# A tuned adaLN block: a third buffer for queries, keys, values and gates, the first projections ahead of the late modulation columns, and new orders on every engine

## The reference

```python
mod = (silu(c) @ wmod).reshape(4, 6, 1, 256)        # shift, scale, gate, twice
sa, ca, ga, sb, cb, gb = mod[:, 0], ..., mod[:, 5]  # ga and gb kept away from 0
h = layernorm(x) * (1 + ca) + sa
q, k = rope(h @ Wq.T), rope(h @ Wk.T)               # 4 heads of 32
v, g = h @ Wv.T, silu(h @ Wg.T)                     # 4 heads of 64
# retention: causal, with decay gamma per head, state S (32 x 64) per head
o = rms_norm_per_head(retention(q, k, v)) * gnorm_w
x = x + ga * ((o * g) @ Wo.T)
h = layernorm(x) * (1 + cb) + sb
x = x + gb * (fwht(silu(h @ W1.T) * (h @ W3.T)) @ W2.T)   # hidden width 1024
```

## Time and profile before

| | us |
|---|---|
| median of 3 runs | 286.54 |
| lowest and highest | 286.5, 286.86 |
| the profiled execution, its own time | 287.58 |
| its span, first to last instruction | 285.4 |
| TensorE busy in the span | 258.5 (91%) |
| VectorE, GpSimd, ScalarE busy | 173.6, 138.1, 122.0 |

### The profile page before, as it was taken

How to read it: one execution, slowest core, us unless ns; L and a number is a source line. 1 busy time by engine, 2 the same in 40 slices (tenths; PEclk the granted TensorE clock), 3 DMA queues, 4 the chain that set the end, 5 groups by cost and what they waited for, 6 DMA issues and landing times.

```text
span 285.4 us, 5010 instructions
## 1 busy us (share of the span) xinstructions
PE 258.5 (91%) x1888; PEld 240.7 (84%) x1888; DVE 173.6 (61%) x340; ACT 122.0 (43%) x249; POOL 138.1 (48%) x159
## 2 busy tenths in 40 slices
PE   1696797789999999999999999999998999899992
PEld 1564585679889989999999998999998999799992
DVE  2317777899696675747476786658458555572210
ACT  2414545476247324723473146623454344233320
POOL 2066226415745491474728383755166627542632
PEclk9999689999999999999999999999999999999998
DMA  6997300100010002000200002000100011001011
GB/s 191 383 379 271 147 2 1 37 3 0 2 37 1 2 0 57 20 2 1 75 1 2 0 0 76 0 3 0 40 32 5 2 37 39 0 0 39 5 34 37
DMA packets 11294, 14.02 MB, mean 49 GB/s; under 512 B 1156, under 2 KB 9220, under 8 KB 11016
## 3 DMA queue, kind: packets, MB, share of 16 engines
q1 hardware_dynamic: 11272, 13.71, 14.5%
HBM read 9.77 MB, written 2.11 MB: 42 GB/s over the span
## 4 chain that ended last, share of the span: by engine, by line
PE 68%; DVE 11%; POOL 8%; issue 4%; DMA 4%; ACT 2%; SPq 2%; POOLq 0%; DVEq 0%; ACTq 0%
PE pu L298 25%; PE pacc L298 13%; PE pd L298 5%; PE pa L298 4%; PE pb L298 4%; DMA wmod_sb<-wmod 3%; PE pc L305 3%; DVE xn L622 2%; PE pc L298 2%; POOL rso L784 2%; PE pacc L348 2%; POOL qk L809 1%; POOL hid_lo L830 1%; PE pstate L298 1%; PE pstate L323 1%
## 5 line engine op out<-in xcount | busy, mean ns | idle before, releaser
L298 PE MATMUL pu<-h_hi,w_hi 128*128 128x256 f32 x256 | 73.1, 286 | 0.0
L298 PE MATMUL pu<-h_hi,w_lo 128*128 128x256 f32 x256 | 72.4, 283 | 0.0
L298 PE MATMUL pu<-h_lo,w_hi 128*128 128x256 f32 x256 | 72.4, 283 | 0.0
L830 POOL TENSOR_TENSOR hid_lo<-hid,hid_hi 128x512 fp32r<-128x512 f32 x32 | 43.1, 1350 | 34.9 <-ACT hid_hi L772 34.8
L298 PEld LDWEIGHTS pu<-h_hi,w_hi 128*128 128x128 f32 x256 | 49.0, 191 | 0.4
L298 PEld LDWEIGHTS pu<-h_lo,w_hi 128*128 128x128 f32 x256 | 49.0, 191 | 0.3
L298 PEld LDWEIGHTS pu<-h_hi,w_lo 128*128 128x128 f32 x256 | 49.0, 191 | 0.0
L298 PE MATMUL pacc<-w_hi,hid_hi 128*128 128x256 f32 x128 | 37.6, 294 | 0.7 <-POOL hid_lo L830 0.7
L298 PE MATMUL pacc<-w_lo,hid_hi 128*128 128x256 f32 x128 | 36.2, 282 | 0.0
L298 PE MATMUL pacc<-w_hi,hid_lo 128*128 128x256 f32 x128 | 36.1, 282 | 0.0
L767 ACT ACTIVATE silu<-pu 128x512 f32<-128x512 f32 x32 | 19.0, 594 | 31.6 <-PE pu L298 31.2
...
## 6 DMA issues: line engine op xcount, KB each, us to landing
...
```

The costliest lines, as they stand in the source:

```text
L298: mm = pe.matmul(ps, a, c, start=start and n == 0, stop=stop and n == len(ops) - 1, skip_group_check=True)
L830: pool.tensor_tensor(hid_lo[:, k % 2], hid32[:, k % 2], hid_hi[:, k % 2].bitcast(F32), ALU.subtract).then_inc(p_hid.sem, 1)
```

## The change

`E_BUFS = 3` buffers for `k_hi`, `k_lo`, `v2`, `gg` and `qkt`, indexed by `buf = u % E_BUFS`; ScalarE's waits go to readers of unit u-3. Room is made by four edits: `rope_a` is gone (VectorE writes into `qk`, and GpSimd adds `rope_b` in place; the waits for the readers of the unit before go from GpSimd's `rope` to VectorE's), `y0` is gone (`yo` is scaled in place, after the square is taken), `sq` shares memory with `tmp`, and the block mask of the state shrinks from 256 columns to 4, read as a broadcast. Among the loads, the second part of `wmod` goes behind `w2`, the constants and the second rotation table. The orders of all five engines are rewritten.

```diff
+E_BUFS = 3
-C_CAUSAL, C_HADAMARD, C_BLOCKS, C_END = 0, P, 2 * P, 2 * P + HEADS * DV
+C_CAUSAL, C_HADAMARD, C_BLOCKS, C_END = 0, P, 2 * P, 2 * P + HEADS
     "SP": steps(
-        "0:rows 1:qb 2:qb 3:qb 0:out 1:out 4:qb 5:qb 2:out 6:qb 3:out 7:qb 4:out 5:out 6:out 7:out"),
+        "0:rows 1:qb 2:qb 3:qb 4:qb 5:qb 6:qb 0:out 7:qb 1:out 2:out 3:out 4:out 5:out 6:out 7:out"),
     "PE": steps(
-        "0:cols 0:ht 0:cols.1 0:rows 0:qk 0:vg 0:qkt 0:vg.1 0:sc 0:sc.1 1:ht 0:had 0:st 0:had.1 0:o 1:qk 1:vg "
+        "0:cols 0:ht 0:qk 0:vg 0:rows 0:cols.1 0:qkt 0:vg.1 0:sc 0:sc.1 1:ht 0:st 0:had 0:had.1 1:qk 0:o 0:st.1 "
...
-        rope_a, rope_b, qk = (sb(n, [P, 2, QK]) for n in ("rope_a", "rope_b", "qk"))
-        v2 = sb("v2", [P, 2, 2, HEADS, 2, DV], F32R)
+        qk, rope_b = (sb(n, [P, 2, QK]) for n in ("qk", "rope_b"))
+        v2 = sb("v2", [P, E_BUFS, 2, HEADS, 2, DV], F32R)
...
-        yo, y0, sq, tmp, xn2 = (sb(n, [P, 2, D]) for n in ("yo", "y0", "sq", "tmp", "xn2"))
+        yo, tmp, xn2 = (sb(n, [P, 2, D]) for n in ("yo", "tmp", "xn2"))
+        sq = tmp
...
             load_x(1)
+            sp.dma_start(raw_w2[:], w2).then_inc(in_w2.sem, 16)
+            sp.dma_start(cst[:], consts).then_inc(in_cst.sem, 16)
+            sp.dma_start(trig_sb[:, 1], trig[:, 1]).then_inc(in_trig[1].sem, 16)
             sp.dma_start(wmod_sb[:, :, 2 * D:6 * D], wmod[:, :, 2 * D:6 * D]).then_inc(in_mod2.sem, 16)
-            sp.dma_start(cst[:], consts).then_inc(in_cst.sem, 16)
-            sp.dma_start(raw_w2[:], w2).then_inc(in_w2.sem, 16)
...
-                    if u >= 2:
-                        act.wait_ge(t_o.sem, t_o.after(u - 2, 1))
+                    if u >= E_BUFS:
+                        act.wait_ge(t_o.sem, t_o.after(u - E_BUFS, 1))
```

More of the change, by code:

```diff
@@ L276, in step @@
                         sp.dma_start(qb[rows, :, :, h, :].rearrange("p e t i -> p (e t) i").bitcast(F32),
-                                     qkt[rows, par, :, :, 0].rearrange("p e t i -> p (e t) i").bitcast(F32)
+                                     qkt[rows, buf, :, :, 0].rearrange("p e t i -> p (e t) i").bitcast(F32)
                                      ).then_inc(s_qb.sem, 16)
@@ L396, in step @@
                         pe.wait_ge(d_br.sem, d_br.after(u - 1))
-                    three(pz[k][:, :], [((qkt[:, par, 0, k, 1], qkt[:, par, 1, k, 1]),
+                    three(pz[k][:, :], [((qkt[:, buf, 0, k, 1], qkt[:, buf, 1, k, 1]),
                                          (qb[:, 0, k], qb[:, 1, k]))]).then_inc(t_s.sem, 1)
@@ L405, in step @@
                         pe.wait_ge(d_cols.sem, 2)
-                    three(pstate[:, 0:HEADS * DV], [((k_hi[:, par, k], k_lo[:, par, k]),
-                                                     (v2[:, par, k, :, 0], v2[:, par, k, :, 1]))],
+                    three(pstate[:, 0:HEADS * DV], [((k_hi[:, buf, k], k_lo[:, buf, k]),
+                                                     (v2[:, buf, k, :, 0], v2[:, buf, k, :, 1]))],
                           start=(t == 0)).then_inc(t_kv.sem, 1)
@@ L413, in step @@
                         pe.wait_ge(p_s.sem, states(u, k))
-                        three(out_k[:, :, 0], [((qkt[:, par, 0, k, 0], qkt[:, par, 1, k, 0]),
+                        three(out_k[:, :, 0], [((qkt[:, buf, 0, k, 0], qkt[:, buf, 1, k, 0]),
                                                 (s_hi[:, (t - 1) % 2], s_lo[:, (t - 1) % 2]))], stop=False)
@@ L418, in step @@
                     for h in range(HEADS):
-                        pe.matmul(out_k[:, h], p_hi[:, k, h], v2[:, par, k, h], start=(t == 0 and h == 0), stop=False,
+                        pe.matmul(out_k[:, h], p_hi[:, k, h], v2[:, buf, k, h], start=(t == 0 and h == 0), stop=False,
                                   skip_group_check=True)
-                        mm = pe.matmul(out_k[:, h, 0], p_lo[:, k, h], v2[:, par, k, h, 0], start=False,
+                        mm = pe.matmul(out_k[:, h, 0], p_lo[:, k, h], v2[:, buf, k, h, 0], start=False,
                                        stop=(h == HEADS - 1), skip_group_check=True)
@@ L554, in step @@
                     dve.wait_ge(a_vg.sem, a_vg.after(u, k))
-                    split(d_vlo, v2[:, par, k, :, 1], heads(pa[:, 0:D]), v2[:, par, k, :, 0])
+                    split(d_vlo, v2[:, buf, k, :, 1], heads(pa[:, 0:D]), v2[:, buf, k, :, 0])
                 elif kind == "qklo":
                     dve.wait_ge(a_qkt.sem, a_qkt.after(u))
-                    split(d_qklo, qkt[:, par, 1].rearrange("p t q n -> p (t q n)"), pb[:, :],
-                          qkt[:, par, 0].rearrange("p t q n -> p (t q n)"))
+                    split(d_qklo, qkt[:, buf, 1].rearrange("p t q n -> p (t q n)"), pb[:, :],
+                          qkt[:, buf, 0].rearrange("p t q n -> p (t q n)"))
                 elif kind == "qb" and u == 0:
@@ L564, in step @@
                         rows = slice(h * DK, (h + 1) * DK)
-                        ins = dve.tensor_copy(qb[rows, 1, :, h, :], qkt[rows, par, 1, :, 0].bitcast(F32))
+                        ins = dve.tensor_copy(qb[rows, 1, :, h, :], qkt[rows, buf, 1, :, 0].bitcast(F32))
                     ins.then_inc(d_qb0.sem, 1)
@@ L697, in step @@
                     act.wait_ge(t_vg.sem, t_vg.after(u, k))
-                    if u >= 2:
-                        act.wait_ge(t_o.sem, t_o.after(u - 2, 1))
-                        act.wait_ge(p_y0.sem, p_y0.after(u - 2, 1))
-                        act.wait_ge(t_kv.sem, states(u - 2, 0) + 2 - (u - 2) % 2)
-                    act.activation(v2[:, par, k, :, 0], heads(pa[:, 0:D]), ACT.Copy)
-                    act.activation(gg[:, par, k], pa[:, D:2 * D], ACT.Silu).then_inc(a_vg.sem, 1)
+                    if u >= E_BUFS:
+                        act.wait_ge(t_o.sem, t_o.after(u - E_BUFS, 1))
+                        act.wait_ge(p_y0.sem, p_y0.after(u - E_BUFS, 1))
+                        act.wait_ge(t_kv.sem, states_through(u - E_BUFS))
+                    act.activation(v2[:, buf, k, :, 0], heads(pa[:, 0:D]), ACT.Copy)
+                    act.activation(gg[:, buf, k], pa[:, D:2 * D], ACT.Silu).then_inc(a_vg.sem, 1)
                 elif kind == "qkt":
                     act.wait_ge(t_qkt.sem, t_qkt.after(u))
-                    if u >= 2:
-                        act.wait_ge(t_o.sem, t_o.after(u - 2, 1))
-                    act.activation(qkt[:, par, 0].rearrange("p t q n -> p (t q n)"), pb[:, :], ACT.Copy
+                    if u >= E_BUFS:
+                        act.wait_ge(t_o.sem, t_o.after(u - E_BUFS, 1))
+                    act.activation(qkt[:, buf, 0].rearrange("p t q n -> p (t q n)"), pb[:, :], ACT.Copy
                                    ).then_inc(a_qkt.sem, 1)
@@ L714, in step @@
                         rows = slice(h * DK, (h + 1) * DK)
-                        ins = act.activation(qb[rows, 0, :, h, :], qkt[rows, par, 0, :, 0].bitcast(F32),
+                        ins = act.activation(qb[rows, 0, :, h, :], qkt[rows, buf, 0, :, 0].bitcast(F32),
                                              ACT.Copy)
@@ L739, in step @@
                     if u:
-                        act.wait_ge(d_ss.sem, d_ss.after(u - 1, k))
+                        act.wait_ge(d_x1.sem, d_x1.after(u - 1))
                     act.activation(sq[:, k], yo[:, k], ACT.Square).then_inc(a_sq.sem, 1)
@@ L818, in step @@
                 elif kind == "ss":
-                    pool.wait_ge(d_o.sem, d_o.after(u, k))
-                    if u:
-                        pool.wait_ge(t_yt.sem, t_yt.after(u - 1))
-                    pool.tensor_tensor(y0[:, k], yo[:, k], gg[:, par, k], ALU.mult).then_inc(p_y0.sem, 1)
+                    pool.wait_ge(a_sq.sem, a_sq.after(u, k))
+                    pool.tensor_tensor(yo[:, k], yo[:, k], gg[:, buf, k], ALU.mult).then_inc(p_y0.sem, 1)
                     pool.wait_ge(d_ss.sem, d_ss.after(u, k))
```

50 lines of the change are left out of this document (25 added, 25 removed), and 90 rows, old and new, of the table ORDERS.

## The result

| | before | changed |
|---|---|---|
| median of 4 runs, us | 286.52 (286.5 to 286.86) | 276.21 (275.44 to 276.75) |
| ratio to before, 95% interval | | 0.963 (0.9609 to 0.9651) |
| profiled execution, its own time | 287.58 | 275.44 |
| its span | 285.4 | 273.5 |

The profiled span is 11.9 shorter.

A forecast was written before the change was run, and what follows sets the result against it. TensorE, busy for 91% of the span, was taken as the bound, with time to win mostly in the first 60 us. The terms -2.2 - 1.5 - 1.0 = -4.7 gave 281.8 us, range 278.2 to 285.2.

The forecast's parts named there:

- which stay: From qkt to the first scores: 4.78 us, made of ScalarE's and VectorE's copies, would stay unchanged.
- at the same price: After the first scores: the clock falls again, costing some 3.3 us as before; bounds -3.3 and +3.3.
- 2.95 in all, and no more is to be had: After the first up: TensorE's four remaining waits, 0.59, 0.37, 0.85 and 1.14 us, limit the gain.
- Part 1: Start until the first scores: -2.2 us, scores at 27.9 instead of 30.05.
- near 20.6: At the start: the clock rises there, during rows and cols.1, so qkt begins at 23.1; bounds 22.0 and 25.5.
- Part 2: From the first scores to the first up: -1.5 us, bounds 0 and -2, from fewer waits.
- in one piece, 2.9 us: Ahead of the first scores: TensorE pauses once, from near 25.0 until 27.9, so the clock is expected to fall.
- Rival B: After the first scores: the clock doesn't fall, 278.5 us; chance 20%.
- Part 3: From the first up to the end: -1.0 us, two waits gone for -2.0, against new ones; bounds -2.95 and +2.
- two new waits: Between qkt and sc of unit 5 and between proj and h2t of unit 2: less cover, +0.5 us each.
- rival D: Scores of units 3 to 5: block-query transfers late, three stalls, 288.4 us at 2.2 each; chance 8%.
- The in-place output: Among the memory edits: changes no count or size of a product, its readers are done earlier; 0 us.

The follow-up runs named there:

- e1: The changed kernel with two buffers instead of three, all orders, loads and memory edits kept: 277.18 us, 0.9667 of before.
- e8: The changed kernel with the late modulation columns moved behind unit 0's second vg, VectorE's part behind its copies, GpSimd's butterflies ahead of kspl: 276.19 us, 0.9647 of before.
- e9: The changed kernel run again unchanged: 276.42 us, 0.9657 of before.
- e6: The kernel before, with only GpSimd's second round of w2 butterflies moved ahead of its rotation: 285.43 us, 0.9956 of before.
- e7: The changed kernel, with GpSimd's second round of butterflies held back until VectorE's remainder of unit 0's queries is done: 279.45 us, 0.9746 of before.
- e5: The kernel before, with 14 extra products filling TensorE's three pauses ahead of the first scores: 287.17 us, 1.0022 of before.
- e11: The kernel before with one edit, yo scaled in place, so GpSimd's product waits for ScalarE's square: 288.59 us, 1.0058 of before.
- e12: The kernel before with the new orders from qkt of unit 5 on, on every engine but SyncE: 287.55 us, 1.001 of before.
- e4: The changed kernel with before's orders and loads up to the first up, and the new orders behind it: 283.21 us, 0.9874 of before.
- e2: The changed kernel's three buffers and memory edits with before's orders and order of loads: 287.67 us, 1.0037 of before.
- e13: As e12, with ScalarE's and VectorE's part of unit 5's queries also as far ahead as in the changed kernel: 283.26 us, 0.9853 of before.
- e10: As e8, with VectorE's gates also moved behind the values' remainder: 278.28 us, 0.9703 of before.
- e14: The changed kernel with two buffers and y0 back, so GpSimd's product no longer waits for the square: 276.01 us, 0.9607 of before.

## Where the prediction held, and which of its steps failed

The prediction was wrong in its size. The direction and the mechanism of the three parts held, but 276.21 us lies below the range, and in the profiles the gain is 11.9 us, where the sum has 4.7. Three terms failed: the copies ahead of the first scores, "which stay", shrank by 1.4; the low clock, expected again "at the same price" of 3.3, did not come, and costs 1.6 where it does; and of the waits after the first `up`, "2.95 in all, and no more is to be had", 3.6 was had.

**What held.** `ht` stood at 9.32 (9.7 forecast), `qk` at 13.01 (13.3) with starts 0.21 apart, `vg` ended near 18.4 (18.5) at the low clock, and the late `wmod` was hidden. The third buffer is worth nothing (e1). "qkt, on which the scores hang, still stands behind both groups that were overtaken" was the right brake, and e8 shows the next one behind it, VectorE.

**Part 1: -4.6 instead of -2.2.** Three terms were off. The first, 0.3, is the landing of the first weights (5.92 against 6.19), which differs from run to run by more than that. The second, 0.7, is the rise of the clock. The text took it "near 20.6", as before; it came at 18.5, with the end of `vg`, so both overtaken groups ran at the full clock and `qkt` began at 22.09, at the lower of its two bounds. Even that is no bound: in e9 the products of `vg` start 0.23 apart from 16.18 on, no longer 0.43, and `qkt` is at 21.07. The third, 1.4, failed outright: "made of ScalarE's and VectorE's copies, which stay". They went from 4.78 to 3.37, since GpSimd's last butterfly had ended as the copies began (e6 and e7 show it from both sides). GpSimd's second round stands behind its rotation in both orders. The rotation came 6.0 us earlier (17.96 against 23.96) and the copies only 3.2, so GpSimd was through. What was not asked is which other engine is at work while a timed row runs.

**Part 2: -3.35 instead of -1.5.** The order itself was sized well. Without a low stretch the old orders need 28.5 (e5, e6, e11, e12), the new ones 26.8: -1.75. The rest, 1.6, is the low clock. Two steps of that failed. The pause was to be "in one piece, 2.9 us" and was 1.34, since the copies took 1.4 less; and a long single pause doesn't bring the fall in any case (e7, 3.29 us without one). And the price of 3.3, half of TensorE's busy time at 1.2 GHz, is twice too high: the old orders lose 1.6 in three profiles with the stretch (30.1 to 30.3 against 28.5) and 0.8 in e4, and over 61 executions of before 0.7. Rival B had the event right, and its 278.5 was still too high, because parts 1 and 3 were.

How much of the 1.6 is the change's doing is partly luck. Before's own profile happened to have the stretch, as three other profiles with its start had (e2, e4, e13), but not e6, e11 and e12. Of the eight profiles with the new start only e10 has a fall near the first scores; e7 and e9 have one later, and e9 is the same kernel as the first.

**Part 3: -3.6 instead of -1.0.** "2.95 in all, and no more is to be had" was a wrong bound. It left out a fifth wait, the 0.59 at 257.21 for the norm of unit 7. And the idle column gives less than a stall takes. From the start of the last product ahead to the start of the waiting one, less the usual distance, the five cost 0.76, 0.54, 1.03, 1.31 and 0.75, so 4.4 (an estimate from the trace of before). The forecast let two of them go; all five went. Of the two new waits, +0.5 each, one came where it was forecast, 0.58 at `h2t` of unit 2, and the one at the scores of unit 5 didn't. 4.4 less some 0.8 for the new wait is the 3.6. Here e12 gives the useful half of rival D: the mechanism is real, and its price in e12 is 2.63 us at the scores of unit 5, more than D's 2.2; it doesn't strike in the changed kernel because ScalarE's and VectorE's parts of the queries had been moved ahead of the silu and the norm (e13). The text had credited only VectorE's.

**A term put at 0 that isn't.** "The in-place output" costs 1.55 us in the old orders (e11). The product's readers were looked at, and not what it now waits for. The new orders cover it (e14), so the forecast lost nothing by it.

**What stays open.** The runs don't show why the clock falls where it does, at 27, 31, 50 or 54 us. Neither a single long pause (e7) nor the work just ahead (e9 beside the first profile) tells. Among the seven profiles with before's start and no filled pauses, the moment of the rise does: in the four where the clock had risen by 21.4 us it fell later (before, e2, e4, e13), in the three where it rose after 22.3 it did not (e6, e11, e12). No run set the rise on purpose, so this is a coincidence of seven profiles and not a cause shown. The spread of the changed kernel's times (275.7 to 279.59 in e9) goes in part with the clock: e9's longest execution has the lowest mean of its six, 0.985, but two at 1.0 aren't its shortest.
